# Gated linear attention, MLP and mixture of experts on one core: head sums by TensorE, and a new order at the end of each batch's recurrence

## The reference, cut to what matters

```python
# attention, for each head: a recurrence over the 512 tokens
S = S * exp(g_t)[..., None] + k_t[..., None] * v_t[..., None, :]
o_t = einsum('bhk,bhkd->bhd', q_t, S)
o = (o - mean(o)) * rsqrt(var(o) + 1e-5)      # over the 16 numbers of a head
x = x + (silu(g) * o) @ Wo
x = x + silu(rmsnorm(x) @ W1) * (rmsnorm(x) @ W3) @ W2
# experts: top 4 of 16 by softmax(xn @ router), weights renormalised
y = sum(w_e * (silu(xn @ gate_e) * (xn @ up_e)) @ down_e)
out = x_in + s * silu(y)                      # s: the attention layer's output
```

## Time and profile before

| | us |
|---|---|
| median of 3 runs | 540.68 (539.45 to 542.52) |
| the profiled execution | 540.49 |
| its span, from the first to the last instruction | 538.8 |
| busy: TensorE matmuls | 440.8 |
| busy: DVE | 310.2 |
| busy: POOL | 291.6 |
| busy: ACT | 232.3 |

### The profile page before, as it was taken

The page is one execution under the profiler, slowest core; times in us unless marked ns, Lnnn a source line. Parts: engine busy times, 40 slices in busy tenths (PEclk is TensorE's granted clock), DMA queues, the critical chain, the costliest instruction groups (busy, mean ns, idle before and its releaser), DMA issues.

```text
span 538.8 us, 8832 instructions
## 1 busy us (share of the span) xinstructions
PE 440.8 (82%) x2189; PEld 260.3 (48%) x2190; DVE 310.2 (58%) x591; ACT 232.3 (43%) x527; POOL 291.6 (54%) x221
## 2 busy tenths in 40 slices
PE   2879863164978978895999899999999999999665
PEld 2333420031325434542654667767767767777422
DVE  5887779986998699754546533333333333333107
ACT  3556753003412231312435345655655556555402
POOL 5338883315888888887000026666656666666600
PEclk9999985575989998999799999999999999999968
DMA  8755689756444444439749167666667767664495
GB/s 247 235 182 182 241 319 342 291 155 224 152 159 151 141 170 129 145 94 371 260 138 261 42 169 117 110 106 108 112 102 115 110 99 116 107 107 57 55 278 205
DMA packets 73417, 90.30 MB, mean 168 GB/s; under 512 B 7752, under 2 KB 56488, under 8 KB 73384
## 3 DMA queue, kind: packets, MB, share of 16 engines
q1 hardware_dynamic: 53848, 66.05, 39.2%
q0 software_dynamic: 14448, 19.34, 21.2%
q10 hardware_dynamic: 5088, 4.50, 2.7%
HBM read 50.66 MB, written 39.21 MB: 167 GB/s over the span
## 4 chain that ended last, share of the span: by engine, by line
PE 52%; DVE 17%; issue 9%; DMA 8%; POOL 8%; ACT 3%; another core or an unknown queue 2%; SPq 0%; ACTq 0%; DVEq 0%; POOLq 0%
PE mm_ps L322 28%; PE sum_ps L322 12%; DVE st L1037 4%; DMA vrep<-v_scratch 4%; POOL qs L573 4%; PE turn_ps L1357 3%; DVE kv L1029 3%; POOL rows_scratch L608 3%; PE mm_ps L1464 3%; DMA y_scratch<-y,X 3%; PE mm_ps L1503 1%; PE sum_ps L1335 1%; PE turn_ps L1503 1%; DMA xn<-in_L_attn_x_dram 1%
## 5 line engine op out<-in xcount | busy, mean ns | idle before, releaser
L642 POOL DMA_INDIRECT y_scratch<-y,X x79 | 123.0, 1557 | 135.3 <-ACT y L876 85.9
L573 POOL TENSOR_TENSOR qs<-st,q_sb 128x1024 f32<-128x1024 f32 x32 | 75.5, 2358 | 54.2 <-DVE st L1037 46.0
L322 PE MATMUL mm_ps<-w_gu,xT 128*128 x474 | 102.5, 352 | 1.6 <-DVEq L1247 1.6
L1165 DVE TENSOR_TENSOR xT<-turn_ps,xT 128x256 f16<-128x256 f32 x79 | 33.4, 424 | 87.3 <-ACT xT L787 72.4
L322 PE MATMUL mm_ps<-an2T,w 128*128 128x512 f16 x264 | 66.3, 407 | 19.4 <-ACT sg L793 6.9
L322 PE MATMUL sum_ps<-wd,hT 112*128 x316 | 81.3, 380 | 0.0
L1037 DVE TENSOR_TENSOR_SCAN st<-sum_ps,kv 128x512 f32<-128x512 f32 x64 | 75.3, 1211 | 1.1
L608 POOL DMA_INDIRECT rows_scratch<-rows,slot_u x64 | 63.1, 986 | 16.9 <-issue 14.7
L322 PEld LDWEIGHTS mm_ps<-w_gu,xT 128*128 128x128 f16 x474 | 46.0, 97 | 32.7 <-issue 2.9
L1335 PE MATMUL sum_ps<-qs,sumk 128*32 128x512 f32 x128 | 37.5, 676 | 29.5 <-POOL qs L573 29.5
L1252 DVE SCALAR_TENSOR_TENSOR h<-mm_ps,X,sl 128x224 f32<-128x224 f32 x79 | 35.6, 451 | 40.1 <-ACT sl L860 38.2
(11 more groups left out here) (185 smaller groups left out, 515.2 us busy)
## 6 DMA issues: line engine op xcount, KB each, us to landing
vrep<-v_scratch SPq DMA_DIRECT2D x64, 256.0 KB
rows_scratch<-zrow SPq DMA_DIRECT2D x20, 548.0 KB, 7.7
X<-rows_scratch SPq DMA_DIRECT2D x80, 137.0 KB
w_gu<-y_scratch SPq DMA_DIRECT2D x16, 256.0 KB
y_scratch<-zrow ACTq DMA_DIRECT2D x6, 640.0 KB
w_gu<-in_L_ffn_gate_proj_dram SPq DMA_DIRECT2D x16, 224.0 KB, 5.3
w_gu<-in_L_ffn_up_proj_dram SPq DMA_DIRECT2D x16, 224.0 KB, 5.8
wd<-in_L_ffn_down_proj_dram SPq DMA_DIRECT2D x1, 3136.0 KB, 16.8
```

Source lines behind the costliest of these rows:

```text
L322: last = nc.tensor.matmul(out_ap, lhsT, rhs, start=(n == 0), stop=(n == len(pairs) - 1))
L573: nc.gpsimd.tensor_tensor(qs[:, u % 2, :, :], st[:, u % 2, :, :], pair_bc(q_sb[:, TOK(a)]), ALU.mult).then_inc(s["qs_ready"], 1)
L642: nc.gpsimd.indirect_dma_start(y_dram[u % 2], bass.IndirectOffsetOnAxis(ap=X[:, u, TOKEN_C:TOKEN_C + 1].bitcast(U32), axis=0), y[:, u, :], ...
L1165: nc.vector.tensor_tensor(xT[:, u % 2, 1, :, :].rearrange("p c n -> p (c n)"), PS[u % 2][:, 0:KC * P], xT[:, u % 2, 0, :, :].rearrange("p ...
```

## The change

- **Head sums.** ACT squares oT's first half and the bank O0 where it drains the second half, TensorE sums the squares over each head by 8 matmuls with sumk's last 16 columns (they hold KS = 1/4 where the partition belongs to the head), ACT copies the 128x64 sums into ghead, and DVE's root begins with the scaling. TensorE turns oT only when the sums are copied, for they lie in bank T0.
- **Order in step 7 and step 0.** TensorE makes the last readout before the MLP's first product; ACT's SILU of it stands behind the draining. DVE makes the low halves behind recurrence 7 (step 7, not 6), and the first gating in step 0 between recurrences 0 and 1.
- **POOL.** The product of step 5 no longer waits for the row roots, and one scatter moves from step 4 to step 5.
- **SP.** Before the loads of a pair of experts it waits until the pair two before has landed.

```diff
-        sq = sb("sq", [P, TPB, D], F32, att)
+        sq = sb("sq", [P, KC, L], F32, att)
+        HEAD_SUMS = T0[:, 0:TPB * H]
-        HEAD_STEPS = 2 + ROOT_STEPS
-        SCATTERS = (1, 4, 3, 3, 4, 3, 3, 3)
+        HEAD_STEPS = 1 + ROOT_STEPS
+        SCATTERS = (1, 4, 3, 3, 3, 4, 3, 3)
...
             for e in range(E):
+                if e % 2 == 0 and e >= 4:
+                    sp.wait_ge(raw_in[e // 2 - 2], 64)
                 load_gate_up(e)
...
                         pool.wait_ge(s["head_dve"], (b + 1) * HEAD_STEPS)
-                    if u == 5:
-                        pool.wait_ge(s["row_rstd"], b + 1)
                     product(a, u)
...
             def value_half(a, half):
+                if half:
+                    act.wait_ge(s["oT_evac"], a * 2 + 3)
+                    nc.scalar.activation(sq[:, 0, :], oT[:, 0, :], ACT.Square).then_inc(s["sq_ready"], 1)
                 act.wait_ge(s["gla_used"], a * U + (2 + (8 if half else 4)))
                 wait(act, s["tpo_ready"], a * 2)
+                if half:
+                    nc.scalar.activation(sq[:, 1, :], O0, ACT.Square).then_inc(s["sq_ready"], 1)
                 nc.scalar.activation(oT[:, half, :], O0, ACT.Copy).then_inc(s["oT_evac"], 1)
...
-                if c is not None and m < NF:
+                if b is not None and u == 0:
+                    wait(act, s["on_ready"], b * 2)
+                    act.wait_ge(s["head_sums"], b + 1)
+                    nc.scalar.activation(ghead[0][:, :], HEAD_SUMS, ACT.Copy).then_inc(s["sums_out"], 1)
+                if c is not None and 0 < m < NF:
                     gate_silu(c, m)
                 if b is not None:
-                    if u == 0:
-                        wait(act, s["on_ready"], b * 2)
-                        for i in range(2):
-                            act.wait_ge(s["tpo_ready"], b * 2 + (i + 1))
-                            nc.scalar.activation(
-                                sq[:, 2 * i:2 * i + 2, :].rearrange("p t (h d) -> p t d h", d=HD),
-                                PS[i].rearrange("p (t d h) -> p t d h", t=2, d=HD), ACT.Square).then_inc(s["sq_ready"], 1)
...
                     value_half(a, int(u == 7))
+                if c is not None and m == 0:
+                    gate_silu(c, m)
...
                         for _ in recurrence(a, ahead):
                             pass
+                        if ahead == 0 and c is not None:
+                            gated(c, 0)
+                elif c is not None and m == 1:
+                    gated(c, 0)
+                if b is not None and u == U - 1:
+                    for i in range(KC):
+                        dve.wait_ge(s["an2hi_ready"], b * KC + (i + 1))
+                        nc.vector.tensor_tensor(an2T[:, 1, i, :], PS[i], an2T[:, 0, i, :],
+                                                ALU.subtract).then_inc(s["an2lo_ready"], 1)
...
-                        dve.wait_ge(s["sq_ready"], b * 2 + 2)
-                        chain(nc.vector.tensor_reduce(ghead[0][:, :], sq[:, :, :].rearrange("p t (h d) -> p (t h) d", d=HD),
-                                                      AX.X, ALU.add))
-                        chain(nc.vector.tensor_scalar(ghead[0][:, :], ghead[0][:, :], -0.5 / HD, -0.5 * EPS, ALU.mult, ALU.add))
+                        dve.wait_ge(s["sums_out"], b + 1)
+                        chain(nc.vector.tensor_scalar(ghead[0][:, :], ghead[0][:, :], -0.5 / (HD * KS), -0.5 * EPS, ALU.mult,
+                                                      ALU.add))
...
-                if c is not None and m < NF:
+                if c is not None and 0 < m < NF:
                     gated(c, m)
...
+                if b is not None and u == 0:
+                    wait(pe, s["an2lo_ready"], b * KC)
+                    pe.wait_ge(s["sq_ready"], b * 2 + 2)
+                    for t in range(TPB):
+                        for kc in range(KC):
+                            last = nc.tensor.matmul(HEAD_SUMS[:, t * H:(t + 1) * H], sq[:, kc, t * P:(t + 1) * P],
+                                                    sumk[:, P - H:P], start=(kc == 0), stop=(kc == KC - 1))
+                    last.then_inc(s["head_sums"], 1)
-                if c is not None and m < NF:
+                if c is not None and 0 < m < NF:
                     gate_up_mlp(c, m)
                 if a is not None and u > 0:
                     read_out(a, u - 1)
                 if b is not None:
                     if u == 0:
-                        wait(pe, s["an2lo_ready"], b * KC)
+                        pe.wait_ge(s["sums_out"], b + 1)
...
                 if a is not None and u == U - 1:
                     read_out(a, u)
+                if c is not None and m == 0:
+                    gate_up_mlp(c, m)
```

More of the change, by code:

```diff
@@ L249, in build_block @@
             scatter zero_slot zero_row bz_neg wv_mean wv_ready dve_max vt_ready vt_out0 vt_out1 prep_done vr_in0 vr_in1
-            k_bank a_bank kv_ready st_ready qs_ready gla_used oT_evac pool_turn act_turn tpo_ready sq_ready
+            head_sums sums_out k_bank a_bank kv_ready st_ready qs_ready gla_used oT_evac pool_turn act_turn tpo_ready sq_ready
             head_dve on_ready tpb_ready gs_ready og_ready wo_ready xb_ready ms_ready
@@ L1208, in step_fn @@
                         for i in range(2):
+                            dve.wait_ge(s["tpo_ready"], b * 2 + (i + 1))
                             nc.vector.tensor_tensor(
@@ L1224, in step_fn @@
                             .then_inc(s["row_rstd"], 1)
-                    if u == 6:
-                        for i in range(KC):
-                            dve.wait_ge(s["an2hi_ready"], b * KC + (i + 1))
-                            nc.vector.tensor_tensor(an2T[:, 1, i, :], PS[i], an2T[:, 0, i, :],
-                                                    ALU.subtract).then_inc(s["an2lo_ready"], 1)
                 split_low(n - 1)
-                if c is not None and m < NF:
+                if c is not None and 0 < m < NF:
                     gated(c, m)
```

## The result

The kernel after takes 543.32 us (median of 20 runs, 539.36 to 545.5) against 540.73 (20 runs, 539.45 to 543.53): ratio 1.0042, interval 1.0026 to 1.0059. That is a loss of 0.4%, small but clear of the noise. The forecast was 534.5 in a range of 531.3 to 543.0: wrong in sign, and the result lies 0.3 us outside the range. The profiled execution took 544.05, span 542.0 (before 540.49 and 538.8).

What follows compares the result with a forecast made beforehand. Bound by DVE, then POOL and DVE, from 238 us TensorE, with an 11.04 us hole given to no engine. Wo's product moves from 263.0 to 256.6, 6.4 us less: 540.7 - 6.4 = 534.3, say 534.5; range 531.3 to 543.0.

Steps and rivals of the forecast that it cites:

- I take it that the hole goes: The 11.04 us at 245.52 put down to no engine vanish with weights two pairs in flight; bounds 0 and 8.4; chance 0.50.
- price nothing: SP's wait for pair k-2 costs nothing: eight pairs take some 26 us in place of 22, nobody behind it urgent.
- Head sums 1.05: TensorE's eight added f32 matmuls of 16 columns take 1.05 us, between 0.5 and 2.1 (half clock).
- The lock in the first round, gain 0.1: DVE's second head-root step meets POOL's product, so the chain still ends near 109.1: gain 0.1 us, other bound 2.4.
- POOL's freed product, (1,5) at 120.2 and (2,1) at 144.3: First round's pair 5 product moves from 124.65 to 120.2; product (2,1) from 145.96 to 144.3, 1.7 gained of the 5.
- The loop at the border: Readout, first MLP product, gating, second recurrence: 8.1 us from product 7 to product 1, against POOL's 7.3; POOL stands 0.8, plus 1.0 for clock.
- the slower rival's 3.1: Border of rounds 2 and 3: with readout and first product at half clock, POOL stands 3.1, not 1.8; chance 0.12.
- Lead at product (3,7) 1.6: In round 3 POOL's waits of 0.94 and 0.73 go: lead 1.6 us, product (3,7) ends at 236.2.
- 19.4 plus 1.0: Round 4: TensorE work from product (3,7) to Wo is 19.4 us plus 1.0 for the clock; Wo starts at 256.6, before 263.02.
- the hole stays: Rival: the hole stays, ending about when the scatters do, some 1.6 earlier; Wo at 264, 541.7 us; chance 0.25.
- the loop bites: Rival: both borders wholly at half clock and the hole staying, product (3,7) ends at 238.2; 545.5 us; chance 0.12.
- signs of being wrong: Either a hole of 8 us or more still on the chain, or POOL starting product (3,1) after 196.

Runs made afterwards that it cites:

- e14: Kernel before with every expert weight held until all scatters have landed, expert conversion from step 5 of the last round, on a chip with the hole: 546.28 us, ratio 1.0086.
- e15: Kernel after, order of steps 7 and 0 undone, each round 4 scatter waiting until the one before landed, on a chip with the hole: 538.99 us, ratio 0.9956.
- e12: Kernel after, order of steps 7 and 0 undone, without SP's pair waits; expert weights beyond two pairs wait for the last scatter: 536.65 us, ratio 0.9927.
- e1: Kernel before plus only SP's wait for the pair two before, on a chip without the hole: 533.26 us, ratio 1.0017.
- e4: Kernel after with its order in steps 7 and 0 undone, rest of the change kept, on a chip without the hole: 528.45 us, ratio 0.9927.
- e13: Kernel after with only DVE's low halves back in step 6, on a chip with the hole: 543.61 us, ratio 1.0038.
- e16: The kernel of e12 once more, on a chip with the hole: 537.88 us, ratio 0.9916.

## Why the prediction was wrong, point by point

- **"I take it that the hole goes"** failed. It was not the loads' (e14 has it without them). It is made, on some chips, by the scatters issued 1.27 us apart behind the last product, goes when each waits for the one before (e15), and is over 1.0 to 2.6 us behind the last of them in all eleven traces that have it. The argument had taken the busier of two transfers (384 GB/s against 276) for the cause, with the scatters as a condition at most; its own rival had the right remark, that the hole ends about when the scatters do. The Trainium skill (SBUF — State Buffer, SBUF: two separate sides) says that DMA cannot slow a compute operation, by which the hole was not the loads' and had to stay; for the loads e12 agrees with it (TensorE busy 4.65 and 5.00 of 5 us beside 344 and 377 GB/s). What the scatters hold up seems to be the answer to TensorE's work and not the work: the matmuls stand as done in the traces, whose ends of matmuls are modelled, and the engines behind them start late.
- **SP's cap "price nothing"**: 0.17%, 0.9 us, on a chip without the hole (e1).
- **Head sums 1.05**: 1.85, at full clock (1.00 from 190.9 to 192.7 us). The sum counted eight products, as the program has them; the trace shows 16 of 16 columns, 116 ns each, as it shows four for the two f32 matmuls of a readout. Only the turns have one row for each. The bound of 2.1 was meant for half clock, so that it held was luck.
- **The lock in the first round, gain 0.1**: DVE's root met POOL's product as forecast (2.27 us for one step at 104.42), but ended at 108.26, 0.9 earlier than before.
- **POOL's freed product, (1,5) at 120.2 and (2,1) at 144.3**: 119.52 and 144.22, right, with the wait for DVE before (2,1) (3.41) and none before products 2 and 5 of the next rounds.
- **The loop at the border, "8.1 plus 1.0 for the clock, against 7.3", so 1.8**: 2.69. From product 7's end at 185.58, the readout took 1.34 and the product 4.12, together 1.7 over the full-clock sum and not 1.0. The granted clock (the number behind POOL's) fell during the readout and came back before the product's end; columns as in the earlier trace rows, kernel after:
```profile
185.60:187.00 1.40, 1.36 (x5) 0.24 (x6) 0.24 (x1) 0.00 (x0) 1.00 (x1) 0.74 0.52 165
187.00:189.00 2.00, 2.00 (x5) 0.64 (x6) 0.00 (x0) 1.08 (x2) 1.64 (x2) 0.50 0.74 229
189.00:190.00 1.00, 1.00 (x5) 0.40 (x3) 0.00 (x0) 0.31 (x1) 0.97 (x2) 0.66 0.45 149
190.00:191.00 1.00, 1.00 (x7) 0.62 (x6) 0.00 (x0) 0.28 (x1) 1.00 (x1) 1.00 0.24 79
```
So 2.69 lies nearer the slower rival's 3.1, which had both wholly at half and was given 0.12. Its reason against (clock 1.00 with TensorE busy 0.38) stopped one row too early. In the same trace of the kernel before the clock fell in the next microsecond and stayed at 0.50 until 262, under the work behind the hole:
```profile
255.00:256.00 1.00, 0.00 (x0) 0.00 (x0) 0.00 (x0) 0.00 (x0) 0.00 (x0) 0.57 1.04 373
```
- **Lead at product (3,7) 1.6**: 0.9, end 236.91 in place of 236.2.
- **Round 4, "19.4 plus 1.0", without the hole 2.0 behind the old order**: its first parts, readout, product and sums, took 7.0 in place of 5.9 (236.91 to the second product's start at 243.90), 0.8 of it the sums. How the kernel after runs without a hole was not measured: all three times it met a chip that has one. With the hole, 3.5 us more of work than before lie behind it.
- **Which rival was nearest**: "the hole stays" (541.7) with half of "the loop bites" (545.5); 543.32 lies between. Both were held for unlikely. By the prediction's own sum everything but the hole cost 2.0 us, so the forecast's sign hung on the guess about the hole alone. Of its signs of being wrong the hole of 8 us or more came true; product (3,1) at 195.53 stayed ahead of 196.
- **A cost not foreseen, and no large one**: DVE's root of the rows now meets POOL's product of pair 5. One step on 128x4 takes 2.87 us in place of 0.16 (DVE, kernel after):
```profile
169.31 2.87 DVE L269 SCALAR_TENSOR_TENSOR grow<-grow 128x4 f32<-128x4 f32 x1
```
ACT then waits 4.65 for the root. The order undone (e4) has the same product freed and still gains.

## What to carry to other kernels

Where an idle stretch is given to no engine, list everything that begins and ends with it before blaming the largest transfer, and run each alone; here the end of the scatters fitted within 2.6 us each time, and the loads did not. A move that fills one engine's wait can close a loop over three others: add up the whole way round, at the slow clock if the engine has been waiting. And freeing a buffer or dropping a wait is to be timed apart from the reordering that comes with it: here the one gained 0.4 to 0.7% and the other took more than that away.

## What the runs showed of the hardware that was not expected

- The same kernel took 532.1 and 532.2 us on two chips and 541.2 to 541.4 on three others, 1.7% apart, with spreads that don't meet (529.49 to 534.81, 536.74 to 546.42). On the latter the chain of waits has one stretch of 8.2 to 12.4 us given to no engine, or, in e12, e13 and e16, ACT or DVE waits 10.35 to 11.77 us for "remote" and the chain runs through TensorE with 5.0 us of "issue". On the former there is none of it.
- In that stretch TensorE's products are shown done, and the engines that wait for them start 3 to 10 us later (kernel after: head sums done at 244.04, copied at 247.14; product done at 246.65, gated at 255.72). It takes the 13 indirect scatters issued 1.27 us apart behind the last product. With each behind the landing of the one before (4.5 to 7.2 us apart until 263 us, 2.8 to 2.9 from there on) it is gone (e15), at 2.3 to 3.1 times the DMA rate of e14. Whether their spacing counts or how many are under way at once was not told apart. Up to four at 1.27 us between the products of the earlier rounds show no such wait.
- The traces of the chips with the hole also lack records of landed DMA pieces: of 1,024 of the 64 scatters they have 578 to 643 (759 in e15), those of the other chips 1,021 to 1,024. They are short ahead of the hole too (before: 539 of 816 by 237 us) and most in it (55 of 208 behind that). Whether that and the hole have one cause is open, as is why some chips do this and others don't.
- A row of 16 float32 matmuls of 16 columns took 1.85 us at full clock, 116 ns each, and a row of eight turns of 128 columns 1.04 us, 130 ns each.
